# Images 2 and 3 of a fused four-image block: the pixel norm's root is spread early into spare memory, and the residual is scaled in an operand of its own

## The chip, the cores and the metric

One core of one Trainium2 chip runs the whole program. The metric is device time in microseconds (us), median of three runs.

## The reference

The input is `x`, 4 images of 256 channels by 32 x 32 pixels, float32. Four layers follow each other, and each adds to a residual that is kept per image:

1. attention over 1024 queries and 256 keys (8 heads), behind a group norm; its projection is added to x (call the sum x1);
2. a selective scan: group norm, layer norm over channels, depthwise 3 x 3 convolution, silu, a linear recurrence over 1024 pixels, gating, a projection, added (x2);
3. channel attention: group norm, then a layer norm over the 256 channels of each pixel, qkv weights, and 8 heads that attend over channels, not pixels; projection, added (x3);
4. a mix of max pools of sizes 1 to 13 with weights per channel, group norm, added.

Layer 3 is where the change is. Because its attention runs over channels, the whole layer is one 256 x 256 matrix `WE` for an image. With g = GR*x2 + GB the group norm, u = (g - mean over channels) * root the pixel norm (root is 1/sqrt(variance + eps), one number for each pixel), the layer's result is

```
x3[m, pixel] = x2[m, pixel] + BE[m] + sum over c of WE[c, m] * (x2[c, pixel] - GM[c]) * root[pixel]
```

GM is the group's mean; the mean over channels drops out, since the value weights are centred ahead of time. The root depends on the pixel alone, so it may be multiplied in behind the product (before) or ahead of it (after).

## The kernel before, in words

**Layout.** A tensor of an image lies as 128 partitions (channels) x 2 chunks x 1024 pixels. A projection is four blocks `(m, half)` of 128 channels x 512 pixels; a block is 2 float32 products, shown as 4 matmul records, and fills one PSUM bank.

**Streams.** Work is cut into streams: F (group norm, queries, keys), A (attention), C (projection of attention, norms, convolution), B (scan), D (channel attention, layer 3), M (pool layer of images 0 and 1), L and W (pool layer of images 2 and 3: L the small steps, weights and products, W the window maxima). A stream is a Python generator that yields after each step, and runs over the images in turn. A step of image 3 is written here as B3.y1 or D3.out_1_1.

**Order.** On each engine the streams are merged by an order written out by hand or by a search: `PE_ORDER = "F9 A9 F2 ..."` means nine steps of F, nine of A, two of F (`interleave`, line 230). An engine runs its instructions in that order and no other; each step raises a semaphore, and whoever needs it waits for its count. PSUM banks are tables too (`BANKS_D` and the like), one entry for each product; `take` waits until the bank's last reader is done. The SP queue (loads, copies of stacked queries and keys, stores) and POOL have orders of their own.

**Layer 3 of an image (stream D).** DVE normalises x2 to `G`; PE transposes it (xnT0 to 3); DVE takes statistics per pixel (ps0 to 7) and the variance `PVR` (8 numbers on each of 128 partitions); ACT makes the root of it (lines 794 and 797) and the normalised transpose (xnt0 to 7, line 801); PE forms the gram matrix (gram0, gram1, gramT), T1 and the scores A; DVE and ACT do the softmax (lines 1348 to 1374); PE forms PAT and WE (lines 1947, 1955) and BE (be); ACT scales WE's rows (we0, we1, line 823). Then comes the part that changes:

- DVE copies the root to 32 equal columns, into `RB`, a part of the tile T1 that is free by then (rb, line 1381);
- PE forms `CST = WE' GM` (cst, line 1623 called from `attended`), DVE copies it (line 1384);
- PE turns the root to rows with 64 small products (R0, R1, line 1976), and ACT writes them to `R` (r0, r1, line 832), which lies in `HB`, the scratch tile of the pool windows. So R0 waits for the last window of the image before;
- PE forms the four blocks `WE' x2` (line 1665 as XR,BUF); DVE takes each block in two instructions: (block - CST)*R (x3a, line 1396), then + BE + x2 (x3, line 1401), into `PA_`, the pool layer's input. The blocks and x3a wait until the image before has done with `PA_`.

**The pool layer.** Images 0 and 1 do windows and weighted sums on DVE (53 steps of M an image, most of 1.2 to 1.3 us). Images 2 and 3 do windows on DVE (W, 32 steps, two buffers: `PA_` and `PB4`, which lies over the stacked queries `QST` once attention is over) and the weighted sums on PE (L, acc0_0 to acc6_1, line 2075). M1 is filler beside the scan of image 3; W2 is filler beside D3.

**The end.** B3 (scan of image 3) feeds D3, D3 feeds L3 and W3, and the stores close the program. POOL has nine steps: the centring of C (two for each image, line 987) and one fill of `PB4` (line 996).

## Time and profile before

| what | us |
|---|---|
| median of 3 runs (lowest, highest) | 740.16 (739.38, 746.61) |
| the profiled execution, its own time | 742.38 |
| its span, first to last instruction | 740.5 |
| PE busy in the span | 634.9 (86%) |
| DVE busy | 545.4 (74%) |
| ACT busy | 417.8 (56%) |
| POOL busy | 35.5 (5%) |
| mean granted TensorE clock | 0.917 of full |

Busy times of several engines overlap. A small idle time of an engine that is not on the chain costs nothing. The chain of work that ended last says who held the end back; the order in time of one engine's instructions says what stood in front of a given one.

### The profile page before, as it was taken

How to read it: one execution, taken by the hardware profiler on the slowest of the kernel's cores; microseconds unless marked ns; L12 is line 12 of the kernel's file. 1: busy time of each engine (PE TensorE's matmuls, PEld its weight loads, DVE VectorE, ACT ScalarE, POOL GpSimd, SP SyncE). 2: the span in 40 equal slices, each digit the busy share in tenths (PEclk: the TensorE clock that was granted, in tenths of full speed). 3: DMA queues.
4: the chain of work that ended last, by engine and by line, in shares of the span. 5: the costliest groups of instructions: out<-in, count | busy, mean ns of one | idle time of the engine just before them, and what ended most of it. 6: DMA issues, size and time to landing. Idle time of an engine off the chain costs nothing.

```text
span 740.5 us, 9520 instructions
## 1 busy us (share of the span) xinstructions
PE 634.9 (86%) x3472; PEld 303.2 (41%) x3472; DVE 545.4 (74%) x995; ACT 417.8 (56%) x703; POOL 35.5 (5%) x26
## 2 busy tenths in 40 slices
PE   4769996798999979999998897999759659699687
PEld 3545442343333346353543462344315215465332
DVE  3477249523747466857789899987899998999696
ACT  1304644559778658664866795684667754442321
POOL 3300001000002000000030000100020000000000
PEclk9978997799999997999999988999879969899879
DMA  9240141001001220001000400011000001000101
GB/s 322 86 121 2 58 135 29 3 1 28 31 1 57 58 51 2 2 1 58 0 1 1 107 2 1 1 58 57 0 1 1 1 0 58 0 1 1 57 1 57
DMA packets 15855, 26.88 MB, mean 36 GB/s; under 512 B 3601, under 2 KB 7345, under 8 KB 15682
## 3 DMA queue, kind: packets, MB, share of 16 engines
q1 hardware_dynamic: 12512, 22.80, 10.1%
q10 hardware_dynamic: 3298, 3.48, 1.6%
q8 instruction: 28, 0.46, 0.3%
q14 instruction: 17, 0.14, 0.1%
HBM read 14.09 MB, written 4.19 MB: 25 GB/s over the span
## 4 chain that ended last, share of the span: by engine, by line
PE 62%; DVE 19%; ACT 12%; issue 4%; DMA 1%; ACTq 1%; SPq 0%; DVEq 0%
PE PSB L1665 14%; PE PSB L1795 9%; PE PSB L1776 6%; PE PSB L1686 4%; PE PSB L2075 4%; PE PSB L1699 3%; PE PSB L1809 3%; PE PSB L1741 3%; DVE NEGMAX L1185 3%; PE PSB L1761 3%; PE PSB L1909 2%; PE PSB L1876 2%; PE PSB L1841 2%; ACT PT L656 2%; ACT PS L753 2%
## 5 line engine op out<-in xcount | busy, mean ns | idle before, releaser
L1185 DVE TENSOR_REDUCE NEGMAX<-PSB 128x2 f32<-128x512 f32 x128 | 79.5, 681 | 22.8 <-PE PSB L1741 22.6
L656 ACT ACTIVATE PT<-PSB 128x512 f32<-128x512 f32 x128 | 67.4, 606 | 49.2 <-PE PSB L1761 49.0
L1795 PE MATMUL PSB<-XNP,WTAP 64*64 64x512 f32 x576 | 66.8, 616 | 2.6 <-issue 2.6
L1741 PE MATMUL PSB<-KST,QST 96*128 96x256 f16 x256 | 43.4, 320 | 10.8 <-DMA KST<-KL 7.7
L1761 PE MATMUL PSB<-QST,KST 98*128 98x512 f16 x128 | 38.8, 423 | 7.3 <-DMA QST<-ML 6.0
L1795 PEld LDWEIGHTS PSB<-XNP,WTAP 64*64 64x64 f32 x576 | 22.4, 139 | 45.3 <-issue 45.2
L1500 DVE TENSOR_TENSOR PA_<-HB 128x1024 f32<-128x1024 f32 x32 | 39.1, 1223 | 1.3 <-PE PSB L2075 0.6
L987 POOL TENSOR_TENSOR GA<-GA,PT 128x1024 f32<-128x1024 f32 x8 | 20.2, 2540 | 400.2 <-ACT PT L684 400.2
L1741 PEld LDWEIGHTS PSB<-KST,QST 96*128 96x128 f16 x256 | 25.7, 112 | 30.6 <-DMA KST<-KL 8.2
L720 ACT ACTIVATE U<-PSB 64x512 f32<-64x512 f32 x32 | 26.5, 829 | 20.5 <-PE PSB L1795 19.9
L1776 PE MATMUL PSB<-PT,VT 128*32 128x512 f32 x256 | 35.7, 630 | 1.8 <-issue 0.6
L2075 PE MATMUL PSB<-PA_,PT 128*128 128x512 f32 x64 | 33.2, 660 | 4.3 <-ACT PT L915 3.0
L1776 PE MATMUL PSB<-PT,ONES 128*32 128x512 f32 x256 | 34.4, 607 | 0.0
L1495 DVE TENSOR_TENSOR HB<-PA_ 128x1024 f32<-128x1024 f32 x28 | 34.1, 1219 | 0.2
L1699 PE MATMUL PSB<-XF,WDS 128*128 128x256 f32 x128 | 31.3, 403 | 3.1 <-DVE XF L1100 3.1
L1509 DVE SCALAR_TENSOR_TENSOR ACC<-PA_,COEF,ACC 128x1024 f32<-128x1024 f32 x24 | 32.9, 1371 | 0.4
L1164 DVE SCALAR_TENSOR_TENSOR QL<-PSB,QBS,QH 128x512 f16<-128x512 f32 x16 | 11.6, 746 | 26.1 <-ACT QH L631 26.0
L1665 PE MATMUL PSB<-XF,WQ 128*128 128x512 f32 x64 | 29.7, 597 | 0.0
L1665 PE MATMUL PSB<-GA,WP 128*128 128x512 f32 x64 | 29.5, 600 | 0.0
L1665 PE MATMUL PSB<-XR,BUF 128*128 128x512 f32 x64 | 29.1, 597 | 0.0
L1699 PEld LDWEIGHTS PSB<-XF,WDS 128*128 128x128 f32 x128 | 25.4, 201 | 8.5 <-issue 3.2
L1665 PE MATMUL PSB<-PS,WP 128*128 128x512 f32 x64 | 28.8, 598 | 0.0
...
## 6 DMA issues: line engine op xcount, KB each, us to landing
...
```

The source lines that it names most:

```text
L656: e.activation(PROB[:, 4 * kt + j, :], bank("A", b, f"st{g}_{kt}_{j}")[:, :], ACT.Exp)\
L1185: e.tensor_reduce(NEGMAX[:, h, 2 * j:2 * j + 2], bank("A", b, f"s{h}_{j}")[:, :].rearrange("p (t k) -> p t k", t=2), AX.X, ALU.max, negate ...
L1495: e.tensor_tensor(HB[:, 1:1 + H, :], x[:, 1:1 + H, 0:W], x[:, 1:1 + H, 2:2 + W], ALU.max)\
L1500: e.tensor_tensor(y[:, 1:1 + H, 1:1 + W], HB[:, 0:H, :], HB[:, 2:2 + H, :], ALU.max)\
L1509: e.scalar_tensor_tensor(out=acc, in0=interior(PA_, cc), scalar=COEF[:, cc, k:k + 1], in1=acc, op0=ALU.mult, op1=ALU.add).then_inc(*dve_m. ...
L1665: mm = e.matmul(s[:, :], w(cc), src[:, cc, hs(half)], start=(cc == 0), stop=(cc == CC - 1))
L1699: mm = e.matmul(s[:, m * NK:(m + 1) * NK], WDS[:, cc, n % 4, m * P:(m + 1) * P], src, start=(n == 0), stop=(n == 4 * CC - 1))
L1741: mm = e.matmul(s[:, t * NK:(t + 1) * NK], QST[0:96, h, qt * P:(qt + 1) * P], KST[0:96, h, :], start=True, stop=True)
L1761: e.matmul(s[:, :], KST[0:98, h, kt * P:(kt + 1) * P], QST[0:98, h, hs(g % 2)], start=True, stop=True)\
L1776: mm = e.matmul(bank("A", b, f"pv{g}_0", n)[HD * j:HD * j + HD, :], w, PROB[:, 4 * kt + j, :], start=(kt == 0), stop=(kt == 1))
L1795: mm = e.matmul(banks[gi][64 * half:64 * half + 64, :], WTAP[rows, cc, tap(2 * cc + gi, dy, dx), :], XNP[rows, cc, dy + 16 * half:dy + 16 ...
L2075: mm = e.matmul(bank("L", b, f"acc0_{cc}", half)[:, :], DG[:, cc, k, :], POOLED[k % 2][:, cc, 1 + 16 * half:17 + 16 * half, 1:1 + W], star ...
```

## The change

For images 2 and 3 (`LATE = 2`):

- the root is spread to `RBL` and `RL`, two views of the bytes of `QST` behind `PB4`, which are free once the attention of image 3 has read its queries. So R0 and R1 no longer wait for the windows of the image before, and rb, R0, R1, r0, r1 move from behind WE to behind the pixel statistics;
- a new step pair xr0, xr1 on DVE writes (x2 - GM)*RL to `GA0` (free after the convolution input is written), 128 x 1024 each. The product reads `GA0`, and no longer waits for the image before to be done with `PA_`; x3a is gone, x3 takes the block from PSUM and adds BE and x2 in one instruction; cst is gone on PE and DVE;
- images 0 and 1 keep the old steps. The steps get semaphores of their own (streams' labels E and G);
- all four order texts, the SP and POOL orders and all bank tables are written anew, for all images.

The core of the diff:

```diff
+        SPARE = QST[:, :, :].bitcast(f32).rearrange("p a n -> p (a n)")[:, CC * (H + 2) * (W + 2):]
+        RL, RBL = SPARE[:, 0:N], SPARE[:, N:N + QT * HD].rearrange("p (t o) -> p t o", t=QT)
...
 # ACT
             def spread_rows(b):
-                e.wait_ge(*windows(b - 1).at(b - 1, "p6_1"))
+                if b < LATE:
+                    e.wait_ge(*windows(b - 1).at(b - 1, "p6_1"))
+                elif b == LATE:
+                    e.wait_ge(*pe_a.at(B - 1, "st3_1_3"))
+                else:
+                    e.wait_ge(*dve_g.at(b - 1, "xr1"))
...
 # DVE
+            def early_root(b):
+                e.wait_ge(*(pe_a.at(B - 1, "st3_1_3") if b == LATE else pe_g.at(b - 1, "R1")))
+                yield from root_columns(b, RBL)
+            def scaled_residual(b):
+                GM = GN["D"][3]
+                e.wait_ge(*act_g.at(b, "r1"))
+                e.wait_ge(*(act_c.at(B - 1, "xn1") if b == LATE else pe_g.at(b - 1, "out_1_1")))
+                for cc in range(CC):
+                    e.scalar_tensor_tensor(out=GA0[:, cc, :], in0=XRES[b % 2][:, cc, :], scalar=GM[:, cc, 0:1], in1=RL,
+                                           op0=ALU.subtract, op1=ALU.mult).then_inc(*dve_g.step(f"xr{cc}"))
+                    yield
+            def late_out(b):
+                e.wait_ge(*dve_d.at(b, "be"))
+                e.wait_ge(*pools_read(b - 1))
+                for m, half in BLOCKS:
...
+                    e.wait_ge(*pe_g.at(b, f"out_{m}_{half}"))
+                    e.scalar_tensor_tensor(out=PA_[:, lo:lo + 16, 1:1 + W],
+                                           in0=bank("G", b, f"out_{m}_{half}")[:, :].rearrange("p (h w) -> p h w", w=W),
+                                           scalar=BE[:, m:m + 1],
+                                           in1=XRES[b % 2][:, m, hs(half)].rearrange("p (h w) -> p h w", w=W),
+                                           op0=ALU.add, op1=ALU.add,
+                                           accum_out=PART["M"][:, m, half:half + 1]).then_inc(*dve_g.step(f"x3_{m}_{half}"))
...
 # DVE stream_d
                 yield from pixel_stats(b)
+                if b >= LATE:
+                    yield from early_root(b)
                 yield from gram(b)
+                if b >= LATE:
+                    yield from scaled_residual(b)
                 yield from channel_softmax(b)
                 yield from attended(b)
-                yield from block3_out(b)
+                yield from (late_out(b) if b >= LATE else block3_out(b))
...
 # PE stream_d
                 yield from pixel_rows(b)
+                if b >= LATE:
+                    yield from spread_rows(b)
                 yield from gram(b)
                 yield from channel_scores(b)
                 yield from attended(b)
-                yield from spread_rows(b)
-                e.wait_ge(*pools_read(b - 1))
-                yield from project(b, WE, XRES[b % 2], act_d.at(b, "we1"), pe_d, "out_", "D", dve_d, "x3a_")
+                if b >= LATE:
+                    e.wait_ge(*dve_g.at(b, "xr1"))
+                    yield from project(b, WE, GA0, act_d.at(b, "we1"), pe_g, "out_", "G", dve_g, "x3_")
+                else:
+                    yield from spread_rows(b)
+                    e.wait_ge(*pools_read(b - 1))
+                    yield from project(b, WE, XRES[b % 2], act_d.at(b, "we1"), pe_e, "out_", "E", dve_e, "x3a_")
...
-C6 W1 C2
+C7 W1 C1
...
-F5 X1 A3 X1 F3 A3 X1 F3 A3 F3 A2 M1 A1 M5
+F4 X1 F1 A3 F1 X1 F2 A3 F1 X1 F2 A3 F3 A2 M1 A1 M5
```

The order texts say nothing until they are read out step by step. The stretches that the prediction speaks of, read out (in PE's and ACT's lines runs of equal steps are drawn together):

```
PE, start of image 0
 before  F0.k  A0.s0_0 .. s2_0 (9 steps)  F0.vT F0.setup_projections  A0.s2_1 .. s3_3  A0.mT0
 after   F0.k  F0.vT  A0.s0_0 .. s2_1 (10 steps)  F0.setup_projections  A0.s2_2 .. s3_3  A0.mT0
DVE, image 1's first row maxima
 before  C0.x1_1_1 F1.kl0 C0.gn_m1 F1.kl1 F1.vt F2.gn_st0_00 F2.gn_st0_01 C0.gn_gm1 F2.gn_st0_10 C0.gn_gm21 C0.gn_var1
         F2.gn_st0_11 C0.gn_b1 F2.gn_m20 C0.g1_0 A1.mx0_0 A1.mx0_1 C0.g1_1 ... A1.mx3_3 A1.mh0 F2.gn_sq0 A1.ml0
 after   C0.x1_1_1 F1.kl0 F1.kl1 C0.gn_m1 F1.vt C0.gn_gm1 C0.gn_gm21 C0.gn_var1 C0.gn_b1 C0.g1_0 A1.mx0_0 C0.g1_1 ...
         A1.mx3_3 F2.gn_st0_11 A1.mh0 A1.ml0
PE, norm of image 3's scan
 before  C3.proj0_1_1 B2.proj1_0_1 B2.proj1_1_0 B2.proj1_1_1 M1.w1 C3.gn1 M1.w2 D2.gn2 C3.sums1_0 C3.sums1_1
 after   C3.proj0_1_1 B2.proj1_0_1 C3.gn1 B2.proj1_1_0 M1.w1 M1.w2 B2.proj1_1_1 C3.sums1_0 C3.sums1_1 D2.gn2
POOL    before  C2.c1_1  fill  C3.c1_0 C3.c1_1        after  C2.c1_1 C3.c1_0  fill  C3.c1_1
ACT, ahead of image 3's scan
 before  B3.silu B3.v0_0 B3.v0_1 D2.t1 B3.v0_2 B3.v1_0 .. v1_2  B3.ev0 B3.lv0 B3.ev1 B3.lv1
 after   B3.silu B3.v0_0 .. v1_2  D2.r0 D2.r1  B3.ev0 B3.lv0 D2.t1 B3.ev1 B3.lv1
DVE, image 3's scan to its gating (M1 steps are the filler)
 before  B3.y1 D2.arec D2.arok D2.ap0 D2.ap1 M1.t4_1 .. M1.t6_1 (7 steps)  B3.yn0 M1.p6_1 D2.be D2.rb B3.yz0 B3.yn1 B3.yz1
         M1.acc6_1 D2.cst B3.xm0_0 .. xm1_1  D2.x3a_00 ...
 after   B3.y1 D2.xr1 M1.t3_1 D2.ab D2.aok D2.aclip M1.p3_1 D2.amax D2.arow M1.acc3_1 M1.t4_1 M1.p4_1 D2.afill D2.arec
         D2.arok M1.acc4_1 D2.ap0 B3.yn0 D2.ap1 B3.yz0 B3.yn1 B3.yz1 B3.xm0_0 .. xm1_1  M1.t5_1 M1.p5_1 M1.acc5_1 D2.be
         M1.t6_1 B3.ln_var2_0 B3.ln_var2 M1.p6_1 M1.acc6_1 D2.x3_00 ...
PE, image 3's gating to its second residual
 before  B3.yv1 D2.WE D2.be D2.cst D2.R0 D2.R1 B3.op x4  D2.out_0_0 out_0_1 out_1_0  B3.sums2 x2  D2.out_1_1
         B3.proj1_0_0 proj1_0_1 proj1_1_0 L2.gn3 B3.proj1_1_1 D3.gn2 L2.w1 L2.w2
 after   B3.yv1 D2.PAT B3.op x4  D2.WE D2.be B3.sums2 x2  B3.proj1_0_0 D2.out_0_0 out_0_1 B3.proj1_0_1 D2.out_1_0
         out_1_1 B3.proj1_1_0 proj1_1_1 L2.gn3 L2.w1 D3.gn2 L2.w2
PE, image 3's layer 3
 before  D3.xnT x4  L2.acc0_0 acc0_1 acc1_0 acc1_1 acc2_0  D3.gram0 L2.acc2_1 D3.gram1 gramT L2.acc3_0 D3.T1 L2.acc3_1 D3.A
         L2.acc4_0 acc4_1 D3.PAT L2.acc5_0 D3.WE be L2.acc5_1 acc6_0 acc6_1 D3.cst R0 R1 out x4
 after   L2.acc0_0  D3.xnT x4  L2.acc0_1 acc1_0 acc1_1 acc2_0  D3.R0 R1 gram0 gram1 gramT L2.acc2_1 D3.T1 L2.acc3_0 D3.A
         L2.acc3_1 acc4_0 acc4_1 acc5_0 D3.PAT L2.acc5_1 D3.WE be L2.acc6_0 D3.out_0_0 L2.acc6_1 D3.out_0_1 out_1_0 out_1_1
DVE, image 3's layer 3, behind B3.x2_1_1
 before  5 W2 window steps and the group norm's small steps up to D3.g2_1; L2.coef behind g2_1; W2.p6_1 D3.rb D3.cst D3.x3a/x3 x4
 after   8 W2 window steps, L2.coef and the small steps up to D3.g2_1; ... D3.rb ... D3.xr0 W2.t4_1 D3.xr1 ... W2.p6_1 D3.x3 x4
```

## Rows read from the trace of the kernel before

**Rows 1.** The page's chain that ended last, shares of the span by line.

```profile
PE PSB L1665 14%; PE PSB L1795 9%; PE PSB L1776 6%; PE PSB L1686 4%; PE PSB L2075 4%; PE PSB L1699 3%; PE PSB L1809 3%; PE PSB L1741 3%; DVE NEGMAX L1185 3%; PE PSB L1761 3%; PE PSB L1909 2%; PE PSB L1876 2%; PE PSB L1841 2%; ACT PT L656 2%; ACT PS L753 2%
```

**Rows 2.** Stretches: length, busy of PE, PEld, DVE, ACT, POOL, clock, DMA, GB/s.

```profile
380.00:460.00 80.00, 70.87 (x443) 33.99 (x439) 75.89 (x125) 53.95 (x82) 4.57 (x2) 0.91 0.12 26
...
523.80:529.10 5.30, 1.29 (x10) 1.09 (x8) 4.72 (x22) 3.62 (x6) 0.00 (x0) 0.92 0.00 2
529.10:535.10 6.00, 5.96 (x14) 1.91 (x16) 4.84 (x15) 3.18 (x6) 0.00 (x0) 0.50 0.00 0
...
540.00:560.00 20.00, 13.34 (x100) 4.37 (x104) 19.69 (x26) 11.28 (x20) 2.30 (x1) 0.74 0.00 1
```

**Rows 3.** Time order, PE at the start: start, us, what, idle before.

```profile
38.86 4.02 PE L1741 MATMUL PSB<-KST,QST 96*128 96x256 f16 x18 [4.27 <-DMA KST<-KL]
42.67 2.34 PE L1726 MATMUL PSB<-WV,XDS 128*128 128x256 f32 x8
```

**Rows 4.** Time order, DVE, behind image 1's first half of row maxima.

```profile
129.83 1.34 DVE L1056 SCALAR_TENSOR_TENSOR MSQ_F<-STAT_F,MSQ_F 128x8 f32<-128x8 f32 x1
131.09 0.27 DVE L1194 TENSOR_TENSOR ML<-PSB,MH 32x128 f16<-32x128 f32 x1
```

**Rows 5.** Time order, PE, from image 3's attention projection to its convolution.

```profile
518.35 5.31 PE L1665 MATMUL PSB<-PS,WP 128*128 128x512 f32 x12
...
529.14 1.09 PE L1686 MATMUL PSB<-GA,MAT 128*64 128x512 f32 x1 [1.57 <-issue]
...
546.66 1.99 PE L1809 MATMUL PSB<-XNP,IPZ 64*64 64x512 f32 x8 [9.04 <-ACT XNP L708]
```

**Rows 6.** Time order, POOL from 400 on.

```profile
476.01 2.02 POOL L996 MEMSET QST<- 128x2312 f32 x1 [91.44 <-PE PSB L1761]
537.11 5.19 POOL L987 TENSOR_TENSOR GA<-GA,PT 128x1024 f32<-128x1024 f32 x2 [59.08 <-ACT PT L684]
```

**Rows 7.** Groups of DVE and ACT instructions, 540 to 742 and 564 to 640: busy, mean ns.

```profile
L1396 DVE SCALAR_TENSOR_TENSOR PA_<-PSB,CST,HB 128x512 f32<-128x512 f32 x8 | 6.0, 753 | 6.0 <-PE PSB L1665 6.0
L1509 DVE SCALAR_TENSOR_TENSOR ACC<-PA_,COEF,ACC 128x1024 f32<-128x1024 f32 x12 | 15.4, 1282 | 0.2
...
L832 ACT ACTIVATE HB<-PSB 128x512 f32<-128x512 f32 x2 | 1.1, 582 | 0.0
```

**Rows 8.** Time order, DVE, image 3's scan and gating.

```profile
599.76 1.28 DVE L1294 SCALAR_TENSOR_TENSOR U<-U,COL,PS 128x1024 f32<-128x1024 f32 x1
...
618.05 3.33 DVE L1311 SCALAR_TENSOR_TENSOR PS<-PSB,GS,XNP 128x512 f32<-128x512 f32 x4
```

**Rows 9.** Time order, PE, root and blocks of image 2 beside image 3's scan.

```profile
613.38 3.50 PE L1976 MATMUL PSB<-MAT,T 128*32 128x128 f32 x64
...
620.42 5.31 PE L1665 MATMUL PSB<-XR,BUF 128*128 128x512 f32 x12
625.67 0.64 PE L1686 MATMUL PSB<-PS,MAT 128*64 128x512 f32 x1
...
629.25 1.98 PE L1665 MATMUL PSB<-XR,BUF 128*128 128x512 f32 x4
...
636.36 1.96 PE L1665 MATMUL PSB<-PS,WP 128*128 128x512 f32 x4
```

**Rows 10.** Time order, PE, layer 3 of image 3.

```profile
645.61 3.68 PE L1898 MATMUL PSB<-MAT,G 128*128 128x128 f32 x16
...
677.28 1.96 PE L2075 MATMUL PSB<-QST,PT 128*128 128x512 f32 x4 [0.63 <-DVE QST L1500]
...
686.87 0.95 PE L1623 MATMUL PSB<-GM_D,BUF 128*128 128x1 f32 x8
...
689.63 7.13 PE L1665 MATMUL PSB<-XR,BUF 128*128 128x512 f32 x16
```

**Rows 11.** Time order, DVE, end of W2 and of layer 3.

```profile
683.47 1.23 DVE L1500 TENSOR_TENSOR PA_<-HB 128x1024 f32<-128x1024 f32 x1
...
697.59 0.75 DVE L1401 SCALAR_TENSOR_TENSOR PA_<-PA_,BE,XR 128x512 f32<-128x512 f32 x1
```

More of the change, by code:

```diff
@@ L107 @@
 PE_D = """
-gn2 xnT0 xnT1 xnT2 xnT3 gram0 gram1 gramT T1 A PAT WE be cst R0 R1 out_0_0 out_0_1 out_1_0 out_1_1
+gn2 xnT0 xnT1 xnT2 xnT3 gram0 gram1 gramT T1 A PAT WE be
 """
@@ L116 @@
 ln_var3 pb3 pbi gram0 gram1 ab aok aclip anan amax arow afill arec arok
-ap0 ap1 be rb cst x3a_0_0 x3_0_0 x3a_0_1 x3_0_1 x3a_1_0 x3_1_0 x3a_1_1
-x3_1_1
+ap0 ap1 be
+"""
+PE_E = """
+cst R0 R1 out_0_0 out_0_1 out_1_0 out_1_1
+"""
+ACT_E = """
+r0 r1
+"""
+DVE_E = """
+rb cst x3a_0_0 x3_0_0 x3a_0_1 x3_0_1 x3a_1_0 x3_1_0 x3a_1_1 x3_1_1
+"""
+PE_G = """
+R0 R1 out_0_0 out_0_1 out_1_0 out_1_1
+"""
+ACT_G = """
+r0 r1
+"""
+DVE_G = """
+rb xr0 xr1 x3_0_0 x3_0_1 x3_1_0 x3_1_1
 """
@@ L895, in pool_stats @@
                 e.wait_ge(stored, stores_before(b))
-                yield from squares(b, 3, act, [dve_d.at(b, f"x3_{cc}_1") for cc in range(CC)],
+                yield from squares(b, 3, act, [third(b)[2].at(b, f"x3_{cc}_1") for cc in range(CC)],
                                    lambda cc: interior(PA_, cc), lambda cc: ACC[:, cc, :].rearrange("p (h w) -> p h w", h=H))
@@ L1379, in attended, with root_columns @@
                 yield
-                e.tensor_copy(RB[:, :, :], PVR[:, :].unsqueeze(2).broadcast_to([P, QT, HD])).then_inc(*dve_d.step("rb"))
+                if b >= LATE:
+                    return
+                yield from root_columns(b, RB)
+                e.wait_ge(*pe_e.at(b, "cst"))
+                e.tensor_copy(CST[:, :], bank("E", b, "cst")[:, 0:2]).then_inc(*dve_e.step("cst"))
                 yield
-                e.wait_ge(*pe_d.at(b, "cst"))
-                e.tensor_copy(CST[:, :], bank("D", b, "cst")[:, 0:2]).then_inc(*dve_d.step("cst"))
+            def root_columns(b, t):
+                e.tensor_copy(t[:, :, :], PVR[:, :].unsqueeze(2).broadcast_to([P, QT, HD])).then_inc(*third(b)[2].step("rb"))
@@ L1961, in attended @@
                 yield
-                s = take("D", b, "cst", dve_d, "cst")
+                if b >= LATE:
+                    return
+                s = take("E", b, "cst", dve_e, "cst")
                 e.wait_ge(*act_d.at(b, "we1"))
-                columns(s, 0, WE, GN["D"][3][:, :, 0]).then_inc(*pe_d.step("cst"))
+                columns(s, 0, WE, GN["D"][3][:, :, 0]).then_inc(*pe_e.step("cst"))
                 yield
             def spread_rows(b):
+                pe, act, dve, st = third(b)
+                late = b >= LATE
                 for half in range(2):
-                    e.wait_ge(*dve_d.at(b, "rb"))
-                    e.wait_ge(*windows(b - 1).at(b - 1, "p6_1"))
-                    s = take("D", b, f"R{half}", act_d, f"r{half}")
+                    e.wait_ge(*dve.at(b, "rb"))
+                    if not late:
+                        e.wait_ge(*windows(b - 1).at(b - 1, "p6_1"))
+                    s = take(st, b, f"R{half}", act, f"r{half}")
                     for t in range(4):
                         for j in range(4):
-                            mm = e.matmul(s[HD * j:HD * j + HD, t * P:(t + 1) * P], RB[:, 4 * half + t, :], mat("ident"),
-                                          start=True, stop=True)
-                    mm.then_inc(*pe_d.step(f"R{half}"))
+                            mm = e.matmul(s[HD * j:HD * j + HD, t * P:(t + 1) * P], (RBL if late else RB)[:, 4 * half + t, :],
+                                          mat("ident"), start=True, stop=True)
+                    mm.then_inc(*pe.step(f"R{half}"))
                     yield
@@ L2051, in stream_d @@
                 yield from pixel_rows(b)
+                if b >= LATE:
+                    yield from spread_rows(b)
                 yield from gram(b)
```

141 lines of the change are left out of this document (79 added, 62 removed), and 6 rows, old and new, of the table BANKS_B.

## The prediction

> **What bounds the kernel now.** I read the chain that ended last first. No line holds more than 14% of the span and nearly all of it is PE [rows 1]: a long, mixed PE chain with breaks. So I looked where PE waits. From 60 to 520 us it is nearly always busy; the breaks are at the start, at image 1's row maxima, ahead of image 3's convolution, in image 3's scan and at the end. Then I read the engines' instructions in time order around each break.
>
> - Ahead of image 3's convolution PE idles for 9.04 us [rows 5], and before that it does 1.29 us of work in 5.3; the six microseconds that follow run at a granted clock of 0.50, though PE is busy in 5.96 of them [rows 2].
> - From 540 us on DVE is as good as full (19.69 of 20) [rows 2]. What is added there delays something, if only the pool windows that serve as filler.
> - In image 3's layer 3 PE goes without a long break from 645.61 to 696.76 [rows 10]. It ends with WE'GM, the root and the four blocks, and only then can DVE close the layer.
>
> So the change matters in two ways: by its own steps after 545 us, and because the orders of all engines are new, for all images. The profiled execution took 742.38 us (span 740.5), the median is 740.16. I add up differences on the span and take them off the median. About 1% (7.4 us) is what a measurement of this kernel tells from no change: below 732.8 is faster, above 747.6 slower.
>
> **The change, part by part.**
>
> *A, the start.* PE idles 4.27 us for copied keys, and then, nine steps into the scores, does vT for 2.34 us [rows 3]. The new order puts vT into the idle time and one score step in its place: its 2.17 us of PE less 0.45 (4.02 us for nine steps). **-1.7.** Its DVE copy lands in idle time too. Bounds 0 (a maximum is late instead) and -2.2.
>
> *B, image 1's maxima.* Before the second half of the maxima's row can be written at 131.09, a group norm step of image 2 takes 1.34 us in front of it [rows 4]; ML itself takes 0.27 with a similar tile. In the new order it stands behind, and three statistics of image 2 no longer precede image 1's norm. Part of that is lost, as the load of image 2 is now queued on SP between the copies of queries. I take **-1.7**, bounds 0 and -3.
>
> *C, norm of image 3's scan.* PE ends C3.proj0_1_1 at 518.4 in both orders, since the same steps precede it. Now gn1 stands behind three projection blocks (5.31 us from 518.35), and sums1 starts at 529.14 [rows 5]. In the new order one block precedes gn1. The block's sum and its square on ACT end near 520.6, so gn1 is 3 us earlier; two DVE steps of B2 fall in between, and the last B2 block is in front of sums1: start near 526.5, -2.6. PE then has hardly paused, so I take full clock, 3.6 us as in the same product later (625.67 to 629.25) [rows 9] instead of 6.6: -3.0. Against it: the fill of 2.02 us on POOL now stands between the two centring steps of 2.6 [rows 6], half of it under ACT's root; and two squares of D2 and one pass of 1.2 precede the means on ACT: +2.2 together. The convolution starts **3.4 us earlier**, bounds 0 and -6.
>
> *D, up to the scan's end.* r0 and r1 (0.58 each) [rows 7] now stand ahead of ev0, T1's copy (0.6) behind lv0: +0.8 with what the second chunk adds. R0 and R1 lie in the silu wait, where PE has had 5.5 us of gram; gram fits behind v1. On DVE rb and xr0 are paid by three window steps fewer up to y1. y1 ends at 601.0 now [rows 8], at 598.4 then.
>
> *E, up to image 3's x2.* Behind y1 DVE has xr1, six window steps of 1.23 [rows 11] and 2 us of small ones, 10.7 in all; then yn, yz twice (1.28 each), then the four xm in 3.33: xm1_1 ends at 617.8 instead of 621.4 [rows 8]. Here the change itself pays: cst (0.8) and the 3.50 us of R0 and R1 [rows 9] no longer precede the gating products, and the three blocks of 5.31 us that hold back sums2 now follow it. sums2 starts near 619.0, not 625.67. But nearly all this is given back: sums2 (3.6) and then four blocks of D2 and four of B3, 8 x 1.72 = 13.8, end at 636.4; now the last one ends at 638.32 [rows 9]. So x2 of image 3 is only **1.9 earlier**, and x3 of image 2 about 1 us later than now.
>
> *F, the end.* Added on DVE: two xr, 128 x 1024 from SBUF. No row shows one; the nearest is the same instruction on the same shape, 1.282 us; lower bound 1.22 (two-input op), upper 1.5 = two of the half-size from PSUM. Removed: four x3a of 0.753 and cst [rows 7]. DVE ends its windows at 684.7 now [rows 11]; +2.56 for xr and +1 for the late x3, -1.9: 686.4. PE sets the end: its first work is dg0 and acc0_0, 0.65 later against x2 than xnT0 now; it saves cst (0.8) and two waits, 0.9 (the longer is 0.63) [rows 10], because out_0_0 and the products of the windows fill in. The last block ends 1.0 earlier against x2. And x3 comes straight behind it, without x3a: -0.8 on the path, the other three x3a were under PE. Together **-1.8**. Bounds: 0 (the two xr and the late windows hold acc6_1 back) and -5.2 (cst 0.8, R0 and R1 at full clock 1.8, x3a 0.8, and 1.8 for the block that now runs ahead of acc6_1). Behind x3 (697.59 + 0.75) [rows 11] the last 42 us are the same in both.
>
> Sum: A -1.7, B -1.7, E -1.9 (which holds C and D), F -1.8: **-7.1**. The profiled execution would be 735.3, the median **733**.
>
> [...]
>
> **The rivals.**
>
> *R1, sums1 stays at half clock.* The same product at 529 ran at 0.50 behind a pause [rows 2]. If the two short waits ahead of gn1 and w2 are enough, C loses its 3.0 us. Then y1 is at 601.4 and xm, sums2 and x2 follow 3 us later, +1.1 against now: total -4.1, **736**. For it: the same row set, as sums1 follows small steps with pauses. Against it: in the 5.3 us of pause itself 0.92 was still granted, and the new pauses are under 2 us in sum. [...] 0.18.
>
> *R2, more is gained in between.* The middle of the order is new as well; from 380 to 460 PE is busy for 70.9 of 80 us [rows 2]. Half of those waits gone: **729**. 0.20.
>
> *R3, slower.* The place is image 3's scan chain, from 537 to 601. The fill on POOL (2.02), r0 and r1 (1.16) and xr0 (1.28) are new ahead of steps on that chain, 4.5 us. They decide if C does not start sums1 before 529: then nothing covers them, windows are pushed over x2, and with A and B gone the end gives back 1.8 at most: +2.7, **743**; with x3 of image 2 and its windows pushed by two xr more, 746 to 748. 0.14.
>
> *R4, the own steps work, the rest cancels.* A to C nought, D and E about nought, F -1.8: **738.5**. 0.08.
>
> Forecast 0.40.
>
> **How the numbers follow.** Half of the forecast's 0.40 and R2 lie below 732.8, and nothing else: 0.40. Slower than 747.6 only in the tail of R3 and what I have overlooked: 0.07. Within 1%: the rest, 0.53. The range holds R2, the forecast, R1 and R4: 727 to 741; it leaves out R3 and the far side of R2.
>
> **What would show it.** A: vT ahead of 38.9 and the first transposed maximum near 51.8. B: the second row written 3.4 earlier. C: sums1 8 pairs in 3.6 us at clock 1.00 and the convolution at 540 (with A and B); the fill between two centring steps. E: no PE record of line 1976 between 610 and 620, and sums2 well ahead of the old time, but x2 of image 3 gaining less than 3 us against the convolution's start. F: xr at 1.28 us, the last block followed by one DVE instruction of 0.75. It is wrong if a bank, now assigned otherwise, makes PE wait where no step is late, or if the windows of image 2 end later than 684 (688 would move the last three blocks).

## The result, and the profile after

The changed kernel takes 749.92 us (median of 8 runs, 747.09 to 751.4) against 742.7 for the kernel before on the same chip (8 runs, 738.57 to 746.61): ratio 1.0098, 95% interval 1.0065 to 1.0131. That is slower by 1%, clear of the noise, where 733 (727 to 741) was forecast. Its profiled execution took 750.38 us, with a span of 748.6, against 742.38 and 740.5: I explain the difference of the spans, **+8.1 us**, where the sum had said -7.1.

The page after, its busy times and its chain by line [rows 1]:

```profile
PE 635.1 (85%) x3456; PEld 299.9 (40%) x3456; DVE 543.8 (73%) x989; ACT 417.8 (56%) x703; POOL 35.7 (5%) x26
...
PE 59%; DVE 21%; ACT 10%; issue 4%; DMA 3%; SPq 2%; ACTq 0%; DVEq 0%
PE PSB L1745 12%; PE PSB L1856 7%; PE PSB L1875 6%; PE PSB L1779 4%; PE PSB L1821 4%; PE PSB L2166 4%; PE PSB L1889 3%; PE PSB L1989 3%; ACT PT L688 3%; DVE NEGMAX L1227 3%; PE PSB L1841 3%; PE PSB L1766 3%; DVE HB L1571 2%; PE PSB L1921 2%; PE PSB L1956 2%
```

No engine has more to do, so the time went into waits and into products at a lower clock (the mean granted clock of the span is 0.913, 0.917 before). DMA and SP's queue now have 5% of the chain, where they had 1%; but e1 below, with SP's old order, has 5% as well, so these shares do not say where the time was lost. What says it is the time of single steps: a step that both kernels have can be looked up in both traces, and the difference is its lateness against before. The ledger takes seven such landmarks, one at the end of each part of the prediction. proj0_1_1 is the last block of image 3's attention projection, y1 the last DVE step of image 3's scan (us; the landmark's lateness in the profile of the changed kernel, what the part added, what was forecast):

| part | up to | late | added | forecast |
|---|---|---|---|---|
| A start | image 0, first transposed maximum | +1.7 | +1.7 | -1.7 |
| B and the middle | C3.proj0_1_1, end | +6.7 | +5.0 | -1.7 |
| C norm of image 3's scan | convolution, start (554.10) | +7.4 | +0.7 | -3.4 |
| D scan | y1, end (609.5) | +8.4 | +1.0 | +0.8 |
| E gating, sums2, blocks | last block of B3 (648.0) | +9.7 | +1.3 | +0.7 |
| F layer 3 of image 3 | last x3 | +7.8 | -1.9 | -1.8 |
| behind it | end | +8.1 | +0.3 | 0 |

D, E and F, where the change itself works, are within 0.6 us of the forecast. A, B and C are off by 3.4, 6.7 and 4.1 us.

How far can one pair of profiles be trusted? The experiments below give four more profiles whose orders behind 512 us are those of the changed kernel (e1, e2, e3, and e2's kernel again; e2's differs in POOL's alone). E is +1.2 and F -1.8 in all five. C is between 0.75 and 0.76 in the three that have the same POOL order. D is +1.0 in three and -0.5 in two, with the granted clock of that stretch at 0.90 and 0.93. The front is less steady: nine kernels with before's front orders have proj0_1_1 between 2.5 us earlier and 3.8 us later than the profile of before. And before's start was a favourable one: e4, which has the old start, shows the same +1.7 at the first transposed maximum. So the first two lines of the ledger need the medians of the experiments.

**Waits for copied keys.** PE at the first scores of images 1 and 2 after (start, us, what, idle before); at the same places it had waited 2.23 and 1.17 before:

```profile
118.66 4.02 PE L1821 MATMUL PSB<-KST,QST 96*128 96x256 f16 x18 [4.86 <-DMA KST<-KL]
...
281.01 1.03 PE L1821 MATMUL PSB<-KST,QST 96*128 96x256 f16 x4 [5.57 <-DMA KST<-KL]
```

The page's DMA issues say why. The line of the low-query copies has the count, KB each and the median us from issue to landing, before and then after:

```profile
QST<-QL SPq DMA_DIRECT2D x12, 128.0 KB, 2.5
...
QST<-QL SPq DMA_DIRECT2D x12, 128.0 KB, 6.1
```

SP takes about 0.6 us for each copy that it issues here (medians 0.59 to 0.63 in both profiles, the longest 0.87). At image 1 it issued the load of the next image (2 x 512 KB) at 101.29, ahead of the high-query copies, before; now it issues it at 108.98, between the high and the low ones, and the copies behind it land late: 6.1 us after their issue in the median, not 2.5. With SP's old order in the changed kernel (e1) the median is 2.9; in the kernel before with the new one (e11) it is 2.4, and the longer wait shows at image 1 alone. What holds the copies back no trace here shows.

**The norm of image 3's scan.** The order of work here is: PE sums over channels (sums1), ACT makes the root, POOL centres the input in two steps, DVE scales it in two steps (the scan's own norm, written to GA), and the convolution starts. On DVE stand also g2_0 and g2_1, the two steps that normalise x2 of image 2 and have nothing to do with this chain. First DVE before:

```profile
533.30 0.81 DVE L1100 TENSOR_SCALAR G<-XR,GR_D,GB_D 128x1024 f32<-128x1024 f32 x1
...
534.63 0.81 DVE L1100 TENSOR_SCALAR G<-XR,GR_D,GB_D 128x1024 f32<-128x1024 f32 x1
...
542.73 2.36 DVE L1153 TENSOR_TENSOR GA<-GA,PT 128x1024 f32<-128x1024 f32 x2
```

Then PE after [rows 5], POOL after [rows 6] and DVE after:

```profile
523.23 1.96 PE L1745 MATMUL PSB<-GA,WP 128*128 128x512 f32 x4
...
533.06 0.64 PE L1766 MATMUL PSB<-GA,MAT 128*64 128x512 f32 x1
...
548.02 3.65 PE L1978 MATMUL PSB<-MAT,G 128*128 128x128 f32 x16 [10.72 <-DVE G L1142]
554.10 1.98 PE L1889 MATMUL PSB<-XNP,IPZ 64*64 64x512 f32 x8 [2.43 <-ACT XNP L740]
```

```profile
539.91 2.71 POOL L1029 TENSOR_TENSOR GA<-GA,PT 128x1024 f32<-128x1024 f32 x1 [149.74 <-ACT PT L716]
542.57 2.02 POOL L1038 MEMSET QST<- 128x2312 f32 x1
544.55 2.77 POOL L1029 TENSOR_TENSOR GA<-GA,PT 128x1024 f32<-128x1024 f32 x1
```

```profile
541.29 1.35 DVE L1136 SCALAR_TENSOR_TENSOR GB_D<-GM_D,GR_D 128x2 f32<-128x2 f32 x1
542.68 5.20 DVE L1142 TENSOR_SCALAR G<-XR,GR_D,GB_D 128x1024 f32<-128x1024 f32 x2
547.79 0.68 DVE L1549 TENSOR_TENSOR PH<-HB 128x512 f32<-128x512 f32 x1
548.51 1.30 DVE L1559 TENSOR_TENSOR PA_<-HB,PH 128x512 f32<-128x512 f32 x2
549.84 0.43 DVE L1363 BATCH_NORM_STATS2 PST<-PSB 128x6 f32<-128x256 f32 x1
550.18 2.34 DVE L1195 TENSOR_TENSOR GA<-GA,PT 128x1024 f32<-128x1024 f32 x2
```

sums1 runs from 533.06 to 536.7 at full clock (granted 1.00, before 0.55), 3.6 us instead of 6.6, and ends only 1.0 late where proj0_1_1 was 6.7 late: that half of step C came true (-5.7, forecast -5.6). Behind it everything is lost again. POOL starts 2.8 late (it started 1.4 behind the end of sums1, now 3.2) and ends 5.0 late (the fill of 2.0 stands between its two steps). And g2_0 and g2_1 take 2.60 us each in the mean (g2_0 2.46); in all 24 cases before this form took 0.79 to 0.81. The small step ahead of them (GB_D, 128 x 2) is held as well: 1.35 us where it took 0.16 before, ending with POOL's first step (542.64 and 542.62). Only three window steps and a statistic later comes the scan's own norm (550.18), 2.9 us behind POOL's end instead of 0.4.

**Images 2 and 3**, PE: sums2 and its blocks [rows 9], the end of layer 3 [rows 10]; DVE: xr1, and the last x3 [rows 8, 11]:

```profile
630.39 0.64 PE L1766 MATMUL PSB<-PS,MAT 128*64 128x512 f32 x1
...
633.98 1.98 PE L1745 MATMUL PSB<-PS,WP 128*128 128x512 f32 x4
635.80 3.60 PE L1745 MATMUL PSB<-GA,BUF 128*128 128x512 f32 x8
...
644.38 3.60 PE L1745 MATMUL PSB<-PS,WP 128*128 128x512 f32 x8
...
698.36 1.89 PE L2166 MATMUL PSB<-PA_,PT 128*128 128x512 f32 x4
700.08 5.31 PE L1745 MATMUL PSB<-GA,BUF 128*128 128x512 f32 x12
```

```profile
609.39 1.28 DVE L1444 SCALAR_TENSOR_TENSOR GA<-XR,GM_D,QST 128x1024 f32<-128x1024 f32 x1
...
705.43 0.75 DVE L1455 SCALAR_TENSOR_TENSOR PA_<-PSB,BE,XR 128x512 f32<-128x512 f32 x1 [0.96 <-PE PSB L1745]
```

xr takes 1.28 us as assumed. sums2 starts 20.9 us behind y1 (24.6 before, 20.6 forecast), and the eight blocks that follow give nearly all of it back. One DVE instruction follows the last block.

### The profile page after: what moved, and what is told of

Read it like the earlier page. It is cut to its first block, busy times and chain, and to the rows that moved or that the text cites. A ratio compares the mean times of both kernels' runs of the same rounds, so it can differ in the third digit from the quotient of the medians.

```text
span 748.6 us, 9480 instructions
## 1 busy us (share of the span) xinstructions
PE 635.1 (85%) x3456; PEld 299.9 (40%) x3456; DVE 543.8 (73%) x989; ACT 417.8 (56%) x703; POOL 35.7 (5%) x26
## 3 DMA queue, kind: packets, MB, share of 16 engines
q1 hardware_dynamic: 12512, 22.80, 10.2%
## 4 chain that ended last, share of the span: by engine, by line
PE 59%; DVE 21%; ACT 10%; issue 4%; DMA 3%; SPq 2%; ACTq 0%; DVEq 0%
PE PSB L1745 12%; PE PSB L1856 7%; PE PSB L1875 6%; PE PSB L1779 4%; PE PSB L1821 4%; PE PSB L2166 4%; PE PSB L1889 3%; PE PSB L1989 3%; ACT PT L688 3%; DVE NEGMAX L1227 3%; PE PSB L1841 3%; PE PSB L1766 3%; DVE HB L1571 2%; PE PSB L1921 2%; PE PSB L1956 2%
## 5 line engine op out<-in xcount | busy, mean ns | idle before, releaser
L1875 PE MATMUL PSB<-XNP,WTAP 64*64 64x512 f32 x576 | 64.2, 595 | 1.0 <-issue 1.0
L1821 PE MATMUL PSB<-KST,QST 96*128 96x256 f16 x256 | 45.4, 329 | 16.9 <-DMA KST<-KL 14.7
L1821 PEld LDWEIGHTS PSB<-KST,QST 96*128 96x128 f16 x256 | 26.8, 116 | 40.1 <-DMA KST<-KL 15.6
L1571 DVE TENSOR_TENSOR HB<-PA_ 128x1024 f32<-128x1024 f32 x28 | 36.3, 1296 | 0.2
L1841 PEld LDWEIGHTS PSB<-QST,KST 98*128 98x128 f16 x128 | 12.0, 105 | 38.2 <-issue 11.5
```

What stands on the lines that cost most here:

```text
L1571: e.tensor_tensor(HB[:, 1:1 + H, :], x[:, 1:1 + H, 0:W], x[:, 1:1 + H, 2:2 + W], ALU.max)\
L1821: mm = e.matmul(s[:, t * NK:(t + 1) * NK], QST[0:96, h, qt * P:(qt + 1) * P], KST[0:96, h, :], start=True, stop=True)
L1841: e.matmul(s[:, :], KST[0:98, h, kt * P:(kt + 1) * P], QST[0:98, h, hs(g % 2)], start=True, stop=True)\
L1875: mm = e.matmul(banks[gi][64 * half:64 * half + 64, :], WTAP[rows, cc, tap(2 * cc + gi, dy, dx), :], XNP[rows, cc, dy + 16 * half:dy + 16 ...
```

## The experiments

All but e7 were timed in five rounds against the kernel before on the same chip; its medians lay between 741.5 and 743.2 us. Each time is followed by its ratio to before with the 95% interval. Kernels that were timed on different chips are compared by their ratios, and a difference of two kernels is known to within 1 to 3 us either way. In the diffs the order words are the texts', shortened to what changes; "x behind y" moves a step of one stream past others, and banks follow.

**e1: SP's order back, in the changed kernel.**

```diff
-F4 X1 F1 A3 F1 X1 F2 A3 F1 X1 F2 A3 F3 A2 M1 A1 M5
+F5 X1 A3 X1 F3 A3 X1 F3 A3 F3 A2 M1 A1 M5
```

> The changed kernel with SP's order of before: the loads of images 2 and 3 stand ahead of all query copies of the image before, not between the high and the low ones. Theory SP: those two loads (2 x 512 KB) stand in front of the low-query and key copies; in the changed kernel TensorE waited 4.86 and 5.57 us for copied keys of images 1 and 2, before it waited 2.23 and 1.17, so 7 us of waits should fall to about 3.4 and the kernel should win back 2 to 5 us of 749.9: 745 to 748. Theory other: the images' lateness is made elsewhere and a shorter wait for keys turns into a wait for maxima: 749 to 750.5, with the waits for keys shorter.

746.09 us, 1.0060 (1.0034 to 1.0085): 3.8 us won back by the medians, 2.8 by the ratios, 3.1 against e3, which has the new SP order and ran on the same chip. PE waits 3.14 and 1.75 us for the keys. Theory SP holds.

**e11: the same words the other way round, in the kernel before.**

> Kernel before with nothing but SP's order of the changed kernel: the loads of images 2 and 3 between the high and the low query copies of the image before. Theory SP: as e1_sp_old won back 3.8 us by the way back, this loses 3 to 4.5 us: 745.5 to 747; TensorE waits 4 to 5.5 us for copied keys of images 1 and 2 instead of 2.23 and 1.17. Theory interplay: before's other orders hide the later copies, under 1 us lost.

745.58 us, 1.0042 (1.0017 to 1.0068): 3.1 us lost, the wait at image 1 is 5.80 us; at image 2 it stays at 1.21. In this profile the lateness grows by 3.3 us between the first transposed maxima of images 0 and 2, and then not at all: the loss is made once, at image 1. The order costs about 3 us by itself.

**e2: the fill first, in the changed kernel.** The same kernel was timed once more as e16 (its label says "before"; it is the changed kernel).

```diff
-C7 W1 C1
+C6 W1 C2
```

> The changed kernel with POOL's order of before: the 2.02 us fill of the second pool buffer stands ahead of image 3's two centring steps, not between them. Theory fill: centring ends 2.0 us earlier, image 3's convolution starts near 552 instead of 554.1, and 1 to 2 us are kept to the end: 748 to 749. Theory port: what holds the convolution back is VectorE's two normalising steps of image 2 (2.60 us each beside POOL's work, where one took 0.81 before), which stand in front of the scan's own norm; they slow down beside the centring as before: no gain over 0.5 us, 749.5 to 750.5.

> The changed kernel with the fill first once more, as the first time (1.0074, 748.6) it gained 1.3 us over the changed kernel and e12_fill_first gained 2.8 over e4 by the same edit. If the edit is worth the same in both, the ratio is 1.006 to 1.007 again; if the difference was one of the set of runs, it comes out near 1.0055.

748.64 us, 1.0074 (1.0041 to 1.0108), and 747.32, 1.0081 (1.0053 to 1.0110): 1.3 to 1.8 us under the changed kernel's ratio, which by itself isn't clear of the noise. g2_0 and g2_1 took 3.52 us together. The norm came 0.5 us earlier, though the front of this execution was 1.1 later: of the fill's 2.0 us 1.7 were kept up to the convolution, in both profiles of this kernel and more than theory port said.

**e3: the start back, in the changed kernel.**

```diff
 PE
-F10 A10 F1 ...
+F9 A9 F2 ...
```

> The changed kernel with the start of before (all orders up to image 0's first sixteen row maxima, with their banks): the value projection stands behind nine score steps again, not in the idle time ahead of them. Theory clock: the small products of the set-up (6.84 us after, 3.82 before) ran at a granted clock of 0.50 only because TensorE's stretch of scores had begun from a pause; with the old start they run at 0.92 again, and the first transposed maximum stands at 53.5 instead of 55.3: 747.5 to 748.5. Theory own sum (as predicted): the new start is the better one by 1.7: 751 to 752.

749.22 us, 1.0103 (1.0073 to 1.0133): no difference to the changed kernel, neither theory. The small products took 4.10 us, at a granted clock of 0.91, but PE had stood for 4.27 us ahead of the scores here too: that the pause sets their clock no run shows.

**e15: the new start alone, in the kernel before.**

> Kernel before with the changed kernel's start alone (value projection in TensorE's idle time ahead of the first scores; orders and banks of the first sixteen row maxima). Own sum (step A as predicted): 1.7 us faster, ratio 0.9977. Theory clock: what the idle time gives (1.2 us), the small products of the set-up take back, which then run at a granted clock of 0.50 (6.8 us instead of 3.8 to 4.95 in three profiles of the old start): ratio 0.9995 to 1.001.

744.24 us, 1.0030 (1.0003 to 1.0056): 2.4 us slower. The interval excludes the gain of the own sum (0.9977); it reaches down to theory clock's range. PE's small set-up products before, where the value projection stands behind the first scores [rows 3]:

```profile
44.84 0.95 PE L1623 MATMUL PSB<-COL,WP 128*128 128x1 f32 x8
45.72 0.71 PE L1643 MATMUL PSB<-SQX 16*128 16x128 f32 x4
46.36 1.05 PE L1623 MATMUL PSB<-VB,WP 128*128 128x1 f32 x8
47.27 1.11 PE L1649 MATMUL PSB<-WP,MAT 128*128 128x256 f32 x4
```

and in e15, where it precedes the scores:

```profile
39.95 3.22 PE L1708 MATMUL PSB<-KST,QST 96*128 96x256 f16 x20 [3.31 <-DMA KST<-KL]
42.96 1.71 PE L1590 MATMUL PSB<-COL,WP 128*128 128x1 f32 x8
44.60 1.21 PE L1610 MATMUL PSB<-SQX 16*128 16x128 f32 x4
46.57 1.87 PE L1590 MATMUL PSB<-VB,WP 128*128 128x1 f32 x8 [0.76 <-DVE PB L995]
48.30 2.05 PE L1616 MATMUL PSB<-WP,MAT 128*128 128x256 f32 x4
```

The four groups of small products take 3.82 us together before, at a granted clock of 0.94 between 43 and 48 us, and 6.84 us in e15, all at 0.50.

**e4: before's orders up to 512 us (SP's too), the changed kernel's behind it.**

> All four orders and the banks of before for everything that is done by 512 us (to image 1's layer 3, SP's order too), and behind that the orders of the changed kernel with its own steps for images 2 and 3. Theory front: the loss is made in the first 512 us, where images 0 to 2 are already 4 to 7 us late; with the old front and the gain of the new steps the kernel stands at 740 to 744. Theory back: the lateness of the front is mostly made good by 536.7 (where the scan's sums of image 3 end 1.0 late) and the loss is made behind it: 748 to 750.

745.33 us, 1.0044 (1.0023 to 1.0066). Both theories hold in part: about 4 us of the loss lie in the front (4.6 by the medians, 4.0 by the ratios), about 3 behind 512 us (3.0 and 3.3).

**e7: what running beside POOL costs, by itself.** In the kernel before, unused results to spare memory:

```diff
+ at ps2, and again behind pbi:
+ e.tensor_scalar(SPARE, XRES[0][:, 0, :], GR[:, 0:1], GB[:, 0:1], ALU.mult, ALU.add)
+ at ps4, and again behind pbi:
+ e.scalar_tensor_tensor(out=SPARE, in0=XRES[0][:, 0, :], scalar=GR[:, 0:1], in1=XRES[0][:, 1, :],
+                        op0=ALU.subtract, op1=ALU.mult)
```

> Kernel before with four more VectorE instructions on 128 x 1024 tiles, whose output nobody reads: a tensor by two columns (the form of the group norm's last step, 0.81 us in 23 of 24 cases before) and a two-tensor instruction from SBUF (the form of the new xr) while POOL centres image 3, and the same two again after 547 us, when POOL stands still. Theory port: beside POOL's 2.6 us instructions each of them takes longer, up to the rest of the POOL instruction that is under way (2 to 3.4 us in all), and 0.81 and 1.28 us when POOL is idle; the centring itself gets longer by what they hold. Theory order: the 2.60 us of the changed kernel were a wait for something else, and all four take 0.81 and 1.28 us.

DVE and POOL in the probe, in order of time for each engine:

```profile
542.49 1.25 DVE L1325 TENSOR_SCALAR QST<-XR,GR_D,GB_D 128x1024 f32<-128x1024 f32 x1
...
544.34 2.69 DVE L1331 SCALAR_TENSOR_TENSOR QST<-XR,GR_D 128x1024 f32<-128x1024 f32 x1
...
555.38 0.81 DVE L1325 TENSOR_SCALAR QST<-XR,GR_D,GB_D 128x1024 f32<-128x1024 f32 x1
556.23 1.28 DVE L1331 SCALAR_TENSOR_TENSOR QST<-XR,GR_D 128x1024 f32<-128x1024 f32 x1
```

```profile
540.84 5.10 POOL L989 TENSOR_TENSOR GA<-GA,PT 128x1024 f32<-128x1024 f32 x2 [59.06 <-ACT PT L686]
```

Beside POOL 1.25 and 2.69 us, alone 0.81 and 1.28. They end 0.5 and 1.1 us behind the POOL instruction that was under way (its two steps ended at 543.2 and 545.9): I read this as a wait for it that the recorded duration includes. Theory port holds in the times of the four; the centring got no longer by them (5.10 us, before 5.19). This kernel was executed once, for its profile; its time is no measurement.

**e10: the same price on the path.** e4 with a sum as a second output of g2_0 and g2_1; in this form the tile written for image 2 isn't the normalised one, and only the time counts.

```diff
-e.tensor_scalar(out_tile[:, cc, :], dst(cc), GR[:, cc:cc + 1], GB[:, cc:cc + 1], ALU.mult, ALU.add)
+e.tensor_scalar(out_tile[:, cc, :], dst(cc), GR[:, cc:cc + 1], GB[:, cc:cc + 1], ALU.mult, ALU.add,
+                accum_out=QSUM[:, cc:cc + 1])
```

> e4_front_old with one instruction changed: the two steps of image 2 that apply its third group norm (VectorE, tensor by two columns, 2.60 us each beside POOL in e4) also write a sum, which nobody reads. [...] Theory order: the two still take 2.60 us, or the convolution waits for something else: ratio as e4.

744.27 us, 1.0030 (1.0010 to 1.0051). DVE, the two steps beside POOL's fill and second centring step:

```profile
535.67 1.34 DVE L1110 TENSOR_SCALAR_CACHE_REDUCE G<-XR,GR_D,GB_D 128x1024 f32<-128x1024 f32 x1
...
536.94 1.33 DVE L1110 TENSOR_SCALAR_CACHE_REDUCE G<-XR,GR_D,GB_D 128x1024 f32<-128x1024 f32 x1
```

1.34 and 1.33 us instead of 2.60. Of the 2.5 us the convolution kept 1.1. The median is 1.1 lower too, but its interval overlaps e4's, so the time alone doesn't show it.

**e12: e4 with the fill first. e13: e10 with the fill first.**

> e4_front_old with POOL's order of before: the fill ahead of image 3's two centring steps. Theory fill alone: centring ends 1.8 us earlier and the convolution with it: ratio 1.002. Theory port: VectorE's two norm steps of image 2 still meet the centring, and the scan's norm stands behind them, so that most of the 1.8 us is lost again: ratio 1.003 to 1.0045 (in e2_fill_first against the changed kernel it was 0.5 us at the norm).

> e10_one_port and e12_fill_first together. If port and fill are what I mis-sized in step C, the convolution of image 3 starts 3.5 to 4.5 us ahead of e4's, which is what was predicted for it (3.4 us ahead of before, 743.3 against 746.7), and the kernel is as fast as before or 1 to 2 us faster: ratio 0.997 to 1.001. If the convolution then waits for image 2's normalised tile or ScalarE, it gains as e10 alone.

742.5 us, 1.0008 (0.9987 to 1.0029), and 741.54, 0.9998 (0.9977 to 1.0019). The fill is worth 1.7 us at the convolution, and 2.8 by the medians; my theory port had said 1 at most. In e13 the convolution starts 4.1 us ahead of e4's, 2.6 without what its front was earlier; 3.5 to 4.5 had been expected. At the end e13 can't be told from e12.

**e14: e12, with the scan's norm directly behind image 2's.**

```diff
 DVE
-D2.g2_0 D2.g2_1 M1.vp_0 M1.v0_0 M1.v1_0 D2.ps0 C3.n1_0 C3.n1_1
+D2.g2_0 D2.g2_1 C3.n1_0 C3.n1_1 M1.vp_0 M1.v0_0 M1.v1_0 D2.ps0
```

> e12_fill_first with two VectorE steps moved: the scan's own norm (two of 1.2 us) directly behind image 2's two norm steps, ahead of three pool window steps and one statistic of image 2 (in e12 the norm starts at 542.86, though POOL ends at 539.3 and image 2's norm steps at 540.5). Theory queue: that is the rest of step C; the norm and the convolution start 2.0 to 2.3 us earlier and the kernel ends 1.5 to 2.3 us earlier: ratio to before 0.998 where e12 has 1.0008. Theory later wait: the window steps only move behind the norm, image 2's statistics and TensorE's work ahead of the convolution come later, and nothing is left at the end: ratio as e12.

740.25 us, 0.9974 (0.9951 to 0.9997): with the new steps and just faster than before, by theory queue. DVE, then PE:

```profile
535.35 3.52 DVE L1108 TENSOR_SCALAR G<-XR,GR_D,GB_D 128x1024 f32<-128x1024 f32 x2
538.79 2.35 DVE L1161 TENSOR_TENSOR GA<-GA,PT 128x1024 f32<-128x1024 f32 x2
```

```profile
539.02 3.65 PE L1944 MATMUL PSB<-MAT,G 128*128 128x128 f32 x16 [9.05 <-DVE G L1108]
542.77 1.81 PE L1855 MATMUL PSB<-XNP,IPZ 64*64 64x512 f32 x8
```

**e17: four edits in the changed kernel** (e1, e2, e3 and the diff of e14 together).

> The changed kernel with four small edits and all its other orders: SP's order and the start as before, the fill first, the scan's norm of image 3 directly behind image 2's two norm steps. Theory four: the edits are the whole difference to the forecast; they were worth 3.8 (SP), 0 to 2 (start), 1 to 2.8 (fill) and 2.3 us (norm) one by one, 8 to 10 together, from 749 or so: 739 to 741, ratio 0.996 to 0.999. Theory overlap: the edits give back the same microseconds, or the middle of the new orders loses by itself: 742 to 745.

739.4 us, 0.9961 (0.9938 to 0.9984). Four small edits of order turn 1% slower into 0.4% faster: 10.2 us by the ratios, the upper end of theory four's 8 to 10. In its profile the parts read C -3.2 (forecast -3.4), D +1.0 (+0.8), E +0.7 (+0.7), F -1.1 (-1.8): from C on the landmarks lie near where the prediction had put them, though its C had still held the fill. What stays off is A and B, -0.5 together instead of -3.4.

**e5 and e6: with and without the new steps, each in orders fitted to it behind 512 us.** Both have before's front, the fill first and g2_0, g2_1 ahead of POOL. What is particular to e5:

```diff
 PE   B3.fc2 D2.R0 D2.R1 D2.gram0 B3.v0 D2.gram1 ...  D2.be D2.out00 B3.op x4 D2.out01 B3.sums2 x2 D2.out10 D2.out11
 ACT  D2.r0 B3.gate_exp D2.r1 B3.silu ...  B3.ev0 D2.t1 B3.lv0
 DVE  D2.xr0 B3.vmin0 ... D2.xr1 D2.ab D2.aok B3.gs ... B3.scan0 ... D2.arow B3.scan1 ...
```

> The new steps of images 2 and 3 in orders of their own behind 512 us, with before's orders and banks ahead of it: image 2's two normalising steps on VectorE end before POOL starts to centre image 3 (as before), the fill of the pool buffer stands ahead of the centring, the root's copies stand in front of the silu table, and image 2's channel softmax goes on between the scan steps, so that two of its four output blocks fit in ahead of image 3's layer sums. Theory own steps: they take 0.8 us (cst) and 3.5 us (root products) out of TensorE's full stretches for each image and four x3a, and with the port and the fill out of the way nothing eats that up: 3 to 8 us under before, 735 to 740. Theory nought: what they take from TensorE they give to ScalarE and VectorE on the scan's chain, and the kernel stays within 1 us of the one with the old front (745.3) or of before (742.3).

> Kernel before (no new steps), with its own orders behind 512 us rearranged by the same rules as in e5_own_fit. Control for it: what of e5's gain is order alone. Theory own steps: it lies about 3 us over e5_own_fit, the cst and the root products that still precede image 3's layer sums: 738 to 742. Theory nought: as fast as e5_own_fit.

e5 739.52 us, 0.9957 (0.9927 to 0.9988); e6 742.51, 0.9987 (0.9958 to 1.0016). The difference is 3.0 us (1.5 to 4.3, from the 12 runs of each on one chip). That is what the new steps are worth if both orders fit their steps equally well, which no run shows: e6 by itself gained nothing clear on before. ("23 of 24" in e7's expectation is wrong, it was 24 of 24.)

**e8 and e9: the same with the orders of all images.**

> The new steps, with the orders of all four images arranged anew from the start (SP's order and the fill as before). Theory front: the orders ahead of 512 us have as much slack as those behind it; TensorE was busy 70.9 of 80 us from 380 to 460, and stood for row maxima, copied keys and norms elsewhere: 8 to 15 us under e5_own_fit, 722 to 732. Theory full engine: TensorE's 635 us of work and the clock leave no more than 2 us there: 733 to 740.

> Kernel before (no new steps), orders of all four images arranged anew from the start by the same rules as e8_own_all. Control for it. Theory own steps: they are worth 3 us in this pair as they were in e5 against e6 (739.5 and 742.5): 741 to 742. Theory order: with all orders free the old steps find as good a place, and it is as fast as e8: 738 to 739.

e8 738.33 us, 0.9946 (0.9922 to 0.9969); e9 745.07, 1.0058 (1.0031 to 1.0086). "Theory full engine" holds for e8: the front gave 1.2 us on e5, within the noise. e9 fits neither of its theories and is slower than the order it came from, so this pair says more of my rearranging than of the new steps.

**e18: e14 up to the convolution, e5 behind it.**

> The order of e14_norm_first up to the start of image 3's convolution (2.5 us ahead of before there, against the same front), and behind it the order of e5_own_fit (which gained 4.9 us on before between that point and the end), fitted at the seam. Theory additive: 6 to 7.5 us under before, 735 to 736.5, which would beat both kernels and e8_own_all. Theory shared slack: both gains end at the same wait for image 2's windows or for TensorE, and it is no faster than e5 or e14: 738 to 740.

**733.89 us, 0.9898 (0.9867 to 0.9929)**, 6 runs: faster than before by 1.0%, than the changed kernel by 2%, and 1 us below what theory additive said. The two gains add up. At the convolution's input it is 4.2 us early against before (its front 1.7), at the end 9.7.

## Why the prediction was wrong, and where it was right

Three steps of the prediction failed: A, B with the middle, and the second half of C. The first half of C, D, E and F came out as forecast.

- **A failed**: -1.7 was forecast, alone in the kernel before it is +2.4 (e15, interval 0.2 to 4.2). The work was moved rightly: PE idles 3.06 instead of 4.27 us. But the sum had no term for the small products, and I never asked what the moved step had done for them: with vT behind the first scores they ran at a granted clock of 0.74 to 1.00, with vT ahead of the scores at 0.50, once at 0.69 (6.83 to 6.85 us in four of the five profiles with this start, 5.68 in one; 3.82 to 4.95 in the 13 with the old). The profile of before was also a favourable one: from the first scores to the first transposed maximum it has 14.3 us, ten of the 13 have 15.6 or 15.7. With the new start it is 15.4 to 17.1. So the +1.7 in the ledger is not the new start's doing, and in the changed kernel the start decides nothing that could be measured (e3). Shown is that the gain is absent; the size of the loss is not.
- **B failed** (-1.7 with the middle; +5.0). I saw that SP's load had moved between the query copies and took it for a small deduction from B. It is a term of its own: 2.8 to 3.8 us (e1), 3.1 (e11, there all at image 1). Nothing in the middle made up for it; R2, which hoped for that, has no support. The move that B was about did work: the second half of the maxima's row (ML) is written 0.3 us behind the first (133.48, 133.79), not 1.5, so 1.2 us are gained there, less than the wait for keys has cost. The step of 1.34 us that stood in its way ended at 131.17, with POOL, which centred until 131.14, so I take it for a wait as well; moved away from it, it takes 0.16 (143.03).

```profile
126.50 4.64 POOL L987 TENSOR_TENSOR GA<-GA,PT 128x1024 f32<-128x1024 f32 x2 [98.00 <-ACT PT L684]
```

- **C, sums1: right** (-5.7 against -5.6; -4.9 in e4). R1 did not happen.
- **C, behind sums1: failed.** It is settled by the start of the convolution in five kernels with one front, each against before and less the lateness of proj0_1_1 (0.7, -1.1, 0.3, -0.8, -1.4). Where one order was profiled more than once this figure came out the same within 0.02 us (0.75 to 0.76 in the changed kernel, e1 and e3, -0.92 and -0.91 in e2's kernel):

| | e4 | e10 sum | e12 fill | e13 both | e14 fill, norm first | forecast |
|---|---|---|---|---|---|---|
| start of the convolution | +1.5 | +0.5 | -0.2 | -1.1 | -2.5 | -3.4 |
| end, in the same profiles | +2.8 | +3.1 | +2.5 | +0.1 | -3.1 | -3.7 |
| ratio to before | 1.0044 | 1.0030 | 1.0008 | 0.9998 | 0.9974 | |

  I had allowed 2.2 us for POOL's fill and ACT's added passes. Measured from the end of sums1 to the end of POOL's centring it is 4.0: POOL starts 1.8 later than before, and ends another 2.2 later by the fill and a slower step. Another 2.4 us, not in the sum at all, are DVE's: g2_0 and g2_1, which had ended 1.7 us before POOL's start and now begin 2.8 behind it, meet the centring; and the norm stands behind them and three window steps. I had asked of xr alone whether it would run beside POOL. What it costs the two g2 is shown by e7 and e10: the same form took 1.25 us beside POOL and 0.81 alone (e7), and with a sum as second output the two took 1.34 and 1.33 us beside POOL, not 2.60 (e10).
- **D and E: right** within 0.2 and 0.6; for D the closeness is in part luck, as two profiles of the same order have -0.5 instead of +1.0. PAT of image 2 had to wait 2.86 us for AP_ where I had seen no wait. That it cost nothing, because sums2 waits for DVE, is my reading of the order; no run tests it.
- **F: right** (-1.8 in all five profiles of this order, as forecast; -1.2 in e4).
- **R3** named the right place and one of the right prices: the fill, decided by whether C starts sums1 late. But it was sized at +2.7 with A and B at nought, and these were at +6.7. The chance of slower, 0.07, came from adding parts that I had taken for independent gains with bounds of 0. Two of the three bounds ought to have reached to the loss side: one part moved a load in SP's queue, another the work that PE had done before a stretch of small products.

In their profiles e10 and e12 lose behind the convolution what they had won ahead of it. E is +2.2 in both, +0.7 and +0.8 in e13 and e14, and nearly all of the difference lies in one product, the gating product of image 3's scan, which started at half clock in all four (0.50 granted in its first 0.98 us). The first line is e10, the second e13:

```profile
615.09 5.87 PE L1924 MATMUL PSB<-G,OPW 128*128 128x512 f32 x8
...
614.32 4.41 PE L1924 MATMUL PSB<-G,OPW 128*128 128x512 f32 x8
```

From 613 to 621 us the granted clock is 0.59 in e10 and 0.83 in e13. Why it rose later in one than in the other stays open, and so does what of A's 2.4 us is clock and what the later maxima.
